# A transformer block on one core: four edits to the head of its schedule, and new due times for its planner

## The reference

```python
x = x + attention(layernorm(x))    # 16 heads of 8, causal, w_qkv, b_qkv, w_proj, b_proj
x = x + experts(layernorm(x))
# experts: 8 dense experts, all tokens through all of them
weights = p * (p > 0.5),  p = sigmoid(x @ Wg + bg)
h = relu(einsum('td,edh->eth', x, W1) + b1[:, None, :])      # 128 -> 512
out = einsum('te,etd->td', weights, einsum('eth,ehd->etd', h, W2) + b2[:, None, :])
```

## Time and profile before

| | |
|---|---|
| median of 3 runs | 678.09 us (677.23 to 678.21) |
| the profiled execution's own time | 677.06 us |
| its span, first to last instruction | 675.3 us |
| TensorE busy | 652.4 us, 97% |
| VectorE, ScalarE, GpSimd busy | 450.6, 443.2, 339.1 us |
| mean granted TensorE clock | 0.977 of full speed |

### The profile page before, as it was taken

One profiled execution on the slowest core, in us unless ns is written; L12 is line 12 of the kernel. 1 busy time (PEld: TensorE's weight loads), 2 busy tenths in 40 slices (PEclk: granted clock), 3 DMA queues, 4 the chain that ended last, 5 costly groups with the idle time before them and its releaser, 6 DMA issues.

```text
span 675.3 us, 12981 instructions
## 1 busy us (share of the span) xinstructions
PE 652.4 (97%) x4325; PEld 439.9 (65%) x4325; DVE 450.6 (67%) x1019; ACT 443.2 (66%) x857; POOL 339.1 (50%) x445
## 2 busy tenths in 40 slices
PE   4989998999999999999999999999999999999998
PEld 3445565667666766667666766666666766677776
DVE  6757786678676876678676876678576776344343
ACT  2446768667766776667776786667666667646543
POOL 5117444457545654457545654456645554554453
PEclk7958999999999999999999999999999999999999
DMA  5441224220322122220322122221322010100200
GB/s 178 97 138 23 57 47 110 58 57 19 92 64 57 48 58 57 73 57 25 93 56 59 48 58 58 73 58 34 79 54 50 31 34 33 49 33 33 79 31 17
DMA packets 24560, 40.08 MB, mean 59 GB/s; under 512 B 3312, under 2 KB 12920, under 8 KB 24496
## 3 DMA queue, kind: packets, MB, share of 16 engines
q1 hardware_dynamic: 24112, 38.89, 20.8%
q10 hardware_dynamic: 384, 0.38, 0.2%
HBM read 23.46 MB, written 2.23 MB: 38 GB/s over the span
## 4 chain that ended last, share of the span: by engine, by line
PE 90%; DVE 3%; ACT 2%; issue 1%; DMA 1%; POOL 1%; SPq 0%; ACTq 0%; DVEq 0%; POOLq 0%
PE ring L1273 11%; PE y_bank L1398 10%; PE ring L1353 10%; PE ring L1206 9%; PE ring L1208 9%; PE ring L1207 9%; PE y_bank L1405 9%; PE y_bank L1400 9%; PE ring L1280 4%; PE ring L1212 3%; DVE f_buf L1174 1%; PE ring L1295 1%; ACT xn L870 1%; PE ring L1369 1%; PE y_bank L1273 1%
## 5 line engine op out<-in xcount | busy, mean ns | idle before, releaser
L969 ACT ACTIVATE h_hi<-ring 128x512 fp32r<-128x512 f32 x256 | 152.6, 599 | 110.4 <-PE ring L1208 106.7
L937 ACT ACTIVATE pt<-ring 128x512 f32<-128x512 f32 x312 | 171.0, 599 | 53.0 <-PE ring L1273 51.1
L845 POOL TENSOR_TENSOR h_lo<-h_all,h_hi 128x512 fp32r<-128x512 f32 x96 | 123.6, 1288 | 161.4 <-ACT h_all L975 143.1
L1161 DVE SCALAR_TENSOR_TENSOR h_lo<-ring,h_hi 128x512 fp32r<-128x512 f32 x160 | 109.1, 685 | 57.1 <-ACT h_hi L969 57.1
L838 POOL TENSOR_SCALAR_AFFINE_SELECT pt<-pt 128x512 f32<-128x512 f32 x128 | 79.8, 637 | 94.5 <-ACT pt L937 94.3
L1094 DVE CUSTOM_DVE_ANT_0 ring<-causal,ring 128x512 f32<-128x512 bf16 x124 | 83.3, 713 | 51.8 <-PE ring L1273 51.8
L1398 PE MATMUL y_bank<-h_hi,w_lo 128*128 128x512 f32 x256 | 110.8, 433 | 2.7 <-DVE f_buf L1174 2.7
L1206 PE MATMUL ring<-x2T_lo,w_hi 128*128 128x512 f32 x256 | 101.9, 398 | 0.0
L1273 PE MATMUL ring<-stack 32*128 32x384 f32 (+3 forms) x998 | 97.1, 372 | 4.9 <-DMA stack<-nmT 2.9
L1208 PE MATMUL ring<-x2T_hi,w_hi 128*128 128x512 f32 x256 | 101.2, 395 | 0.0
L1400 PE MATMUL y_bank<-h_hi,w_hi 128*128 128x512 f32 x256 | 101.2, 395 | 0.0
(11 more groups left out here) (145 smaller groups left out, 795.8 us busy)
## 6 DMA issues: line engine op xcount, KB each, us to landing
f_buf<-gates SPq DMA_DIRECT2D x32, 512.0 KB, 3.7
stack<-parts SPq DMA_DIRECT2D x95, 128.0 KB
x_in<-in_x SPq DMA_DIRECT2D x8, 256.0 KB, 3.0
f_buf<-in_W SPq DMA_DIRECT2D x2, 1024.0 KB, 7.7
out_x<-f_buf SPq DMA_DIRECT2D x7, 256.0 KB, 2.4
stack<-nmT SPq DMA_DIRECT2D x64, 8.0 KB
stack<-stack SPq DMA_DIRECT2D x28, 16.0 KB
out_x<-f_buf SPq DMA_DIRECT2D x2, 128.0 KB, 1.9
```

The source lines that it names most:

```text
L845: g_.tensor_tensor(h_lo[:, (i * SLOTS + s) % H_RING, :], h_all[:], h_hi[:, (i * SLOTS + s) % H_RING, :].bitcast(F32), ALU.subtract).then_i ...
L937: sc.activation(pt[:, slot, :], b[:], ACT.Exp, scale=SCALE).then_inc(free_sem("ex", i, g, u), 1)
L969: sc.activation(h_hi[:, (i * SLOTS + s) % H_RING, :], bank_of("z", i, s)[:], ACT.Relu).then_inc(s_hhi, 1)
L1161: v.scalar_tensor_tensor(out=h_lo[:, (i * SLOTS + s) % H_RING, :], in0=bank_of("z", i, s)[:], scalar=0.0, in1=h_hi[:, (i * SLOTS + s) % H_ ...
```

## The change

Four edits, and new constants for the planner.

1. ScalarE issues the three b1 transfers ahead of `b_cols`. In the planner b1 costs 1200 and the first half of W1 1900 instead of 600 and 2500.
2. GpSimd's `stackset` waits until VectorE has made the b1 parts and the q and k weights; `vset` stands behind it on GpSimd.
3. W2 is issued by ScalarE, behind the same wait for w1(7), instead of by SyncE.
4. The `warm` products are gone, from the planner and from TensorE's program.
5. `SHIFT` has other values, so the order of the items may differ on every engine and in every sequence.

```diff
-SHIFT = {('act', 'exp', False): 23.0,
-         ('act', 'exp', True): 3.5,
-         ('act', 'nm', False): 15.0,
-         ('act', 'nm', True): -2.5,
-         ('dve', 'klo', False): 4,
-         ('dve', 'merge', False): 8,
-         ('dve', 'merge', True): -2,
-         ('dve', 'qlo', False): 3.0,
-         ('dve', 'smax', False): -4.5,
+SHIFT = {('act', 'exp', False): 25.5,
+         ('act', 'nm', False): 25.0,
+         ('act', 'nm', True): -4.5,
+         ('dve', 'hlo', False): -3,
+         ('dve', 'merge', False): 2,
+         ('dve', 'merge', True): -2.0,
+         ('dve', 'smax', False): -5.0,
          ('dve', 'smax', True): -4,
-         ('dve', 'w1', False): 4.0,
-         ('dve', 'xT', False): 5.0,
-         ('dve', 'yT', True): 7.5,
+         ('dve', 'w1', False): 3.5,
+         ('dve', 'xT', False): 10.0,
          ('pe', 'ex', False): 3.0,
-         ('pe', 'ex', True): -11.5,
          ('pe', 'gate', False): -11.0,
          ('pe', 'k', False): 4.5,
-         ('pe', 'max', False): 12.5,
+         ('pe', 'max', False): 17.0,
+         ('pe', 'max', True): 3.0,
          ('pe', 'pv', False): 4.0,
          ('pe', 'q', False): 3.0,
+         ('pe', 'q', True): 6,
          ('pe', 'v', False): 4.5,
-         ('pe', 'w1', False): 0.5,
+         ('pe', 'w1', False): 6.0,
...
-         ('pool', 'nm', False): 10.5}
+         ('pool', 'causal', False): -4,
+         ('pool', 'causal', True): 9.5}
...
-    put("dma", ("b1", None), -60.5, 600, ("dma", ("wqkv", None)))
-    put("dma", ("w1", 0), -60, 2500, ("dma", ("b1", None)))
+    put("dma", ("b1", None), -60.5, 1200, ("dma", ("wqkv", None)))
+    put("dma", ("w1", 0), -60, 1900, ("dma", ("b1", None)))
...
-    put("sp", ("w2load", None), -8.9, 600, ("pe", ("w1", EXPERTS - 1)))
-    put("dma", ("w2", None), -8, 9000, ("sp", ("w2load", None)))
+    put("act", ("w2load", None), -8.9, 700, ("pe", ("w1", EXPERTS - 1)))
+    put("dma", ("w2", None), -8, 9000, ("act", ("w2load", None)))
...
-    put("pool", ("stackset", 1), -20, 2200, ("pool", ("rs1", 0)))
+    put("pool", ("stackset", 1), -20, 2200, ("pool", ("rs1", 0)), ("dve", ("wqk", None)))
...
-        elif banks == EARLY_RING and free and masks_made:
-            bank = min((n for n in range(banks) if holder[n] is None), key=lambda n: emptied_at[n])
-            order["pe"].append(("warm", bank, turns[bank]))
-            form = "full"
-            idle["pe"] = False
-            at(now + (UNIT_COST // 2 if ("xT", 0) in use else 270), "idle", "pe")
...
-                elif kind == "w2load":
-                    sp.wait_ge(*full("w1", EXPERTS - 1))
-                    sp.dma_start(w2_in[:].rearrange("p a (c d) -> p (a c) d", d=C),
-                                 w2.rearrange("e (c p) d -> p (e c) d", p=P)).then_inc(s_w2, 16)
...
                 elif kind == "stackset":
+                    pool.wait_ge(s_wset, 6)
+                    pool.wait_ge(s_b1, 5)
...
             act.dma_start(wqkv_in[:], w_qkv).then_inc(s_wqkv, 16)
-            act.dma_start(b_cols[:], b_cols_in).then_inc(s_bcols, 16)
             act.wait_ge(s_b1zero, 1)
             for k in range(3):
                 act.dma_start(b1_in[32 * k:32 * k + EXPERTS, :], b1).then_inc(s_b1load, 16)
+            act.dma_start(b_cols[:], b_cols_in).then_inc(s_bcols, 16)
...
+                elif kind == "w2load":
+                    act.wait_ge(*full("w1", EXPERTS - 1))
+                    act.dma_start(w2_in[:].rearrange("p a (c d) -> p (a c) d", d=C),
+                                 w2.rearrange("e (c p) d -> p (e c) d", p=P)).then_inc(s_w2, 16)
...
-                if kind == "warm":
-                    if not warmed:
-                        pe.wait_ge(s_mask, 4)
-                        warmed = True
-                    wait(pe, s_free[w[1]], w[2])
-                    mm(ring[w[1]][:, 0:2 * P], ident16[:], mask16.rearrange("p n k -> p (n k)"),
-                       start=True, stop=True)
-                    continue
```

More of the change, by code:

```diff
@@ L312, in list_schedule @@
     holder, turns, use = [None] * EARLY_RING, [0] * EARLY_RING, {}
-    emptied_at, masks_made = [0] * EARLY_RING, False
     banks = EARLY_RING
@@ L454, in list_schedule @@
         for engine in ready:
-            if engine == "pe" and idle[engine]:
+            if idle[engine] and ready[engine] and engine == "pe":
                 pick_pe(now)
@@ L468, in list_schedule @@
                 holder[emptier[key]] = None
-                emptied_at[emptier[key]] = now
-            if what == "done" and key == ("pool", ("mask", None)):
-                masks_made = True
             for other in opens.get(("turn", key) if what == "turn" else key, ()):
@@ L1281, in scores @@
                        skip_group_check=True).then_inc(full_sem("max", *unit), 1)
-            warmed = False
             for w in ORDER["pe"]:
```

## The result

| | before | after |
|---|---|---|
| median of 7 runs | 678.09 us (677.23 to 679.82) | 682.95 us (680.94 to 687.17) |
| ratio | | 1.0084, 95% interval 1.0062 to 1.0107 |
| the profiled execution's own time | 677.06 us | 683.93 us |
| its span | 675.3 us | 682.1 us |
| granted TensorE clock | 0.977 | 0.972 |

What follows compares the result with a forecast made beforehand. TensorE was taken as saturated from 150 us, so microseconds won before about 100 us arrive whole at the end. 677.06 - 4.8 - 3.1 - 1.75 = 667.4, plus 1.0 for the median: 668.4 us, range 660 to 677.

Steps and rivals of the forecast that it cites:

- edit 5: New order in later groups and the saturated part: 0 us, with 2 us to each side.
- the prediction's own signs of being wrong: Granted clock at 0.50 beyond about 65 us, experts' first product not some 9 us earlier, or saturated part gaining idle time.
- Edits 1 and 2: Start of the kernel: short b1 cast lets q start at 12.8 instead of 17.63, 4.8 us; bounds 1.8 and 5.3.
- Edit 3: Group 0's row of maxima: issue plus landing 4.3 us instead of 7.4, 3.1 us won; bounds 1.0 and 4.4.
- my upper row of 5.3: Landing of `b_cols` beside W1, 5.3 us, used for the row transfers' landing in the lower bound of the gain.
- Edit 4: Group 0's ten exponentials go back to back without constants ahead of scores: 1.75 us; bounds nothing and 3.0.
- The clock: TensorE's clock without constants: costed at nothing, since dense real work came before each rise.
- A: Clock rises later, from 57.5 to 77.9 us, after the first ex units: 17.5 us more, 686; chance 0.13.
- C: Before 41.8 us VectorE sets the ex units, so edit 3 and part of 4 bring nothing: 673.3; chance 0.22.
- B: Clock doesn't fall near 37 us, since the stall behind the rows is gone: 664.5; chance 0.12.
- D: Change does not do what it says, b1 parts as late and W2 still in the way: about 677.5; chance 0.08.

Runs made afterwards that it cites:

- e7: Kernel before with b1 first, late clearing, W2 on ScalarE's queue and constants not issued, all in the old order; 672.60 us, ratio 0.9917.
- e1: Kernel before with only its 84 products of constants not issued, planner's lists unchanged; 675.55 us, ratio 0.9965.
- e2: Kernel before with only b1 issued first and GpSimd's clearing late, old lists and constants kept; 672.99 us, ratio 0.9921.
- e3: Kernel before with only the W2 load moved from SyncE's to ScalarE's queue, old order; 677.23 us, ratio 0.9987.
- e9: Kernel before with b1 first, late clearing and W2 on ScalarE's queue, old order, constants kept; 673.81 us, ratio 0.9928.
- e12: Changed kernel with only the new due time of q of sequence 0 undone; 674.86 us, ratio 0.9954.
- e5: Changed kernel with all due times (SHIFT) of the kernel before, planned without constants; 676.61 us, ratio 0.9975.
- e4: Changed kernel with the constants put back in planner and program (110 of them), new due times kept; 673.94 us, ratio 0.9937.
- e8: Changed kernel planned with 110 constants, which the program then does not issue, new due times kept; 674.65 us, ratio 0.9951.
- e21: Changed kernel with one item, ScalarE's copy of the maxima row of group 1, sequence 1, due 10 us earlier; 673.71 us, ratio 0.9950.
- e13: Changed kernel with ScalarE's nm due time of later sequences back at 15 instead of 25; 673.90 us, ratio 0.9960.
- e28: Changed kernel with a planner edge keeping sequence 0's first expert items behind the last maxima of group 2, sequence 1; copy nm(1,1) late; 678.33 us.
- e31: e21 with a planner edge putting the last two maxima of group 2, sequence 1, behind sequence 0's first expert items; copy nm(1,1) early; 681.56 us.
- e14: e5 with only ScalarE's nm due time of later sequences at the new 25 instead of 15; 695.86 us, ratio 1.0265.

## Why the prediction was wrong

**The failed step is edit 5: "I take 0, with 2 us to each side".** With all four program edits and the old order the kernel takes 672.6 (e7), with the new order 683 to 686. The order costs 10.4 to 13.5 us, and turns a gain of 0.8% into a loss of 0.8%. Of the 14.5 us between forecast and result 10.4 are this step, and 4.2 are edits 1 to 4, which won about 5 us (e7) and not 9.7. The step rested on there being only 2.0 us of idle time of TensorE in 90 to 150 and half a us in each 100 after that the earlier trace rows. That bounds what a better order can win; it says nothing of what a worse one can lose. The change gives 20 due times another value (entries added or taken out among them) and takes an item out of the planner, so the loss needed a bound of its own and had none. Of the prediction's own signs of being wrong two came true: the first product of the experts came 3.4 us earlier (101.32 against 104.77) and not 9, and the saturated part gained idle time.

A bound was in the file. `list_schedule` also returns `SPAN`, the time at which its own simulation ends, and for these kernels it is:

| order | `SPAN`, us | measured, us |
|---|---|---|
| old (before, e1, e2, e3, e7, e9) | 640.7 | 672.6 (e7) |
| e12 | 640.9 | 674.9 |
| e5 | 641.7 | 676.6 |
| e4, e8 | 642.2 | 673.9, 674.7 |
| e21 | 642.8 | 673.7 |
| e13 | 643.0 | 673.9 |
| e28 | 644.3 | 678.3 |
| changed | 649.0 | 683.0 to 686.1 |
| e31 | 649.2 | 681.6 |
| e14 | 661.9 | 695.9 |

The simulation puts the changed order 8.3 us behind the old one (measured 10.4) and e14 20.2 behind e5 (measured 19.3). It parts the orders with the crossing from those without it, before anything runs on the chip; differences below some 4 us it doesn't get right.

**Edits 1 and 2: right in size, the 5.1 us of e2 in part luck.** 4.8 us was forecast for the start of q, the 1.28 us of constants included. In the changed kernel q or k takes over the chain 4.5 us earlier (13.15 for 17.63), much by the steps as written: cast 0.42 (forecast 0.43), q or k at 12.99 (12.8), stack transfers at 17.45 (16.9). b1 landed at 7.95, just beyond the bounds of 6.6 to 7.9, and as the step said it hardly mattered. The late clearing costs nothing that shows. But e2 still issues the constants, so by these steps it should have won 3.5 us. That it won 5.1 goes with the early rise of the clock in its trace, which no step had. In e7, without constants, q starts earlier, at 12.73, but its products stand 0.43 apart, and the next w1 starts at 15.60, 0.2 behind e2's. When this rise comes differs even between executions of one kernel: in the three traces of the changed kernel the second w1 starts at 15.66, 16.66 and 17.24, and they take 681.0, 683.9 and 686.5 us.

**Edit 3: a term mis-sized.** 3.1 us (bounds 1.0 to 4.4) against 0.9 in the median, not to be told from nothing, and 0.2 to 0.4 in the trace. The issue shrank as I wrote, 3.95 to 1.19. The landing I took from w_qkv, 3.2, but it was 6.30, above my upper row of 5.3. Both of my rows were of transfers beside the halves of W1, 1 MB each; here 2 MB had been issued 2.7 us ahead of them (W2 at 27.56, the rows at 30.23 in the changed kernel), the DMA engines' share stays at 1.05 or more from 32 to 36.5, and the rows land at 37.32. The Trainium skill, page "Trainium Kernel Development and Optimization", section "Key Constraints", has only the issue time saved by a second queue, 2.8 us here. The trace agrees that the issue time is saved, and disagrees with that as the gain: of the 2.8 us that the issue saved the landing took 2.4 back.

**Edit 4: right alone, not in the sum.** 1.75 us was forecast for the exponentials back to back, and 1.28 for the constants ahead of q stood under edits 1 and 2: 3.0 together, and 2.5 measured alone (e1). Beside edits 1 to 3 nothing measurable is left (e9 and e7). Adding the terms was the mistake. The rows of e7 and e9 above show the lead shrinking from 3.9 us to 0.9 by 88 us.

**The clock: wrong in shape, small in price.** I had it low to about 52 and wrote that beyond 65 the forecast would fail. In windows of 4 us of the changed kernel:

```profile
32.00:36.00 4.00, 2.15 (x12) 1.07 (x12) 4.00 (x9) 0.00 (x0) 0.00 (x0) 0.61 1.05 289
...
44.00:48.00 4.00, 4.00 (x23) 2.35 (x25) 3.10 (x9) 2.09 (x4) 2.09 (x3) 0.68 0.23 70
...
52.00:56.00 4.00, 2.92 (x17) 1.92 (x17) 2.79 (x15) 3.97 (x10) 3.92 (x7) 0.67 0.38 82
...
64.00:68.00 4.00, 4.00 (x40) 1.97 (x33) 0.49 (x1) 1.85 (x6) 0.04 (x1) 0.62 0.00 0
...
76.00:80.00 4.00, 3.83 (x24) 2.16 (x24) 3.32 (x10) 2.47 (x6) 1.81 (x3) 0.66 0.07 17
```

It falls at about 33 and rises at about 46.5, is low again from 53 to 67 and from 77 to 84, and for 3 us more at about 102, where in the kernel before it was low once after 20 us, from 36.9 to 57.4. The prediction argued that constants didn't hold the clock because it fell at 36.9 although they were used; but between 20 us and that fall a single one stands, at 36.42, so the fall tested nothing. What stands is that the clock stayed low from 42.4 to 49.8 while constants filled the gaps. In the same order e4's executions, with constants, have mean granted clocks of 0.982 to 0.990, and those of e8, without, 0.969 to 0.975: the constants do keep the clock up. That activity keeps it high is what the Trainium skill says, page "TensorE: Matmul & The Clock Gate", section "What's actually happening", and here the trace agrees. But no gain in time shows: 673.94 us with them, 674.65 without. One caution on that column: in the changed kernel it has 1.00 from 12 to 16 us, while the products of q and k stand 0.43 apart, as at the granted 0.52 of the kernel before. So it misses that first stretch at the low clock, and a mean clock without constants is really lower than it reads.

**The rivals.** A gave 686 from a late clock: the number came, the mechanism is ruled out by e7, e8, e13 and e21, which all run without constants and take 672.6 to 674.7. C gave 673.3 for edit 3 and part of 4 bringing nothing, which is about what e2, e9 and e7 measure; but its mechanism is not what hid edit 3, since in e3 TensorE waits for the landing and not for VectorE. B did not happen (the clock fell at 33). D did not either.

**What stays open.** The crossing carries 7 to 8 us at equal mean clock; why the orders differ in that clock, which makes the rest of the 10.3, was not tested. e14, with the same crossing among old due times, costs 19 us: there TensorE goes on idling after sequence 1, 2.4 us in 260 to 340 and 3.5 in 340 to 600 against 0.3 and 1.3 in the changed kernel, but which items do that was not followed. Nor is it known why e5 is 4 us behind e7. That the lead e7 loses is the price of its lower clock between 60 and 90 us (0.83 against 1.00) is argued from the times, not tested. The changed kernel scatters by 6 to 9 us where e7's runs lie within 1.2; its medians of 683, 686 and 684 are one kernel's. The longer executions are those with the lower clock (0.960 at 689.9, 0.977 at 680.9).

The fastest kernels are e7 (672.60), e2 (672.99) and e21 (673.71), 0.5 to 0.8% below the kernel before: the edits to the program with the old order, or with the new due times and one of them put back.

## What to carry to other kernels

A new order of a statically scheduled kernel is an edit like any other, and the saturated stretch shows only that it can't win: bound its loss separately, by looking for the item that feeds the longest chain (here a row of maxima) and for what may be put ahead of it. Compare the end of the planner's own simulation for the two orders first: here it was worth 8.3 of the 10.4 us. When a change consists of program edits and new planner constants, measure the program edits in the old order first. Gains won ahead of the saturated part need not add up: look at a later milestone, not at the place of the edit.

## What the runs showed of the hardware

Two transfers of 8 KB on SyncE's queue, issued in 1.19 us on their own, landed only 6.30 to 6.45 us later beside a 2 MB load on ScalarE's queue, with the DMA engines' share at 1.05 in 32 to 36 us. On the same queue as the load they took 3.95 and 3.93. From their first issue until they were there it is 6.95 and 7.1 us with two queues and 7.35 with one: another queue took 0.3 to 0.4 us off.

The cast of 512 elements took 3.10 us beside a GpSimd clearing and 0.42 without it, a factor of 7 for one instruction. The two other kernels with the early clearing have it long too (3.56 in e1, 3.18 in e3), and in every trace with the late clearing it is 0.42.
